# ScalarE's weight casts ahead of its sixteen copies, and GpSimd's value weights ahead of its sums

## The reference

```
h_q = rmsnorm(layernorm(x)) @ w_q.T      h_k = ctx @ w_k.T      h_v = ctx @ w_v.T
score = softmax(mask(h_q h_k^T + position_bias))
x = x + layernorm(x) + (score h_v) @ w_out.T
```

## Time and profile before

| | |
|---|---|
| median of 3 runs | 1126.73 us (1124.93 to 1127.22) |
| profiled execution, its own time | 1123.38 us |
| its span | 1121.6 us, 17499 instructions |
| TensorE busy | 974.0 us, 87% |
| its weight loads | 826.9 us, 74% |
| VectorE busy | 694.0 us, 62% |
| ScalarE busy | 676.8 us, 60% |
| GpSimd busy | 524.9 us, 47% |
| the sixteen copies (L798) | 1024 copies, 303.1 us |
| chain that ended last | TensorE 49%, ScalarE 16%, issue 13%, GpSimd 11%, VectorE 10% |

### The profile page before, as it was taken

One profiled execution on the slowest core, in us unless ns is written; L12 is line 12 of the kernel. 1 busy time (PEld: TensorE's weight loads), 2 busy tenths in 40 slices (PEclk: granted clock), 3 DMA queues, 4 the chain that ended last, 5 costly groups with the idle time before them and its releaser, 6 DMA issues.

```text
span 1121.6 us, 17499 instructions
## 1 busy us (share of the span) xinstructions
PE 974.0 (87%) x5261; PEld 826.9 (74%) x5261; DVE 694.0 (62%) x1225; ACT 676.8 (60%) x2103; POOL 524.9 (47%) x582
## 2 busy tenths in 40 slices
PE   9899999979888888979888888888897987879998
PEld 8778888867767667767777677776786776657886
DVE  5576665556666566747655565647555555748687
ACT  5786856564656474757655565746655465635565
POOL 2443443563537254744446352745446442403367
PEclk9999999999999899989989989989989989989999
DMA  8142267445662546526553546426643553420101
GB/s 309 62 149 100 95 238 253 175 132 188 205 232 73 199 151 224 173 75 229 201 197 116 201 139 221 137 99 218 215 169 131 188 168 120 128 107 1 30 20 57
DMA packets 61292, 171.71 MB, mean 153 GB/s; under 512 B 6055, under 2 KB 8491, under 8 KB 60988
## 3 DMA queue, kind: packets, MB, share of 16 engines
q1 hardware_dynamic: 61244, 171.11, 44.0%
HBM read 159.56 MB, written 11.53 MB: 153 GB/s over the span
## 4 chain that ended last, share of the span: by engine, by line
PE 49%; ACT 16%; issue 13%; POOL 11%; DVE 10%; DMA 0%; DVEq 0%; POOLq 0%; SPq 0%; ACTq 0%
ACT probs_t L798 9%; PE ps_v L363 5%; PE ps_v L365 4%; PE ps_v L364 4%; PE ps_o L363 3%; PE ps_k L363 3%; PE ps_o L364 3%; PE ps_o L365 3%; PE ps_k L364 3%; PE ps_k L365 3%; PE ps_s L2188 3%; PE ps_q L363 3%; ACT scores L787 3%; PE ps_q L364 3%; PE ps_q L365 2%
## 5 line engine op out<-in xcount | busy, mean ns | idle before, releaser
L798 ACT COPY probs_t<-scores 32x128 f32<-32x128 f32 x1024 | 303.1, 296 | 215.4 <-DVE scores L1612 203.6
L787 ACT ACTIVATE scores<-scores,neg_max 128x128 f32<-128x128 f32 x256 | 99.6, 391 | 128.6 <-DVE neg_max L1598 128.0
L1484 DVE TENSOR_TENSOR acc<-ps_o,acc 128x512 f32<-128x512 f32 x128 | 87.7, 685 | 67.1 <-PE ps_o L365 67.1
L1159 POOL TENSOR_TENSOR wq_lo<-raw_q,wq_hi 128x256 fp32r<-128x256 f32 x65 | 53.6, 825 | 144.5 <-ACT wq_hi L620 144.5
L1594 DVE TENSOR_TENSOR scores<-ps_s,shift 128x512 f32<-128x512 f32 x64 | 44.3, 691 | 119.0 <-PE ps_s L2188 115.7
L363 PE MATMUL ps_o<-wo_hi,att_hi 128*128 128x512 f32 x256 | 106.4, 416 | 7.0 <-DVE acc L1484 5.2
L363 PE MATMUL ps_v<-wv_hi,ct_hi 128*128 128x256 f32 x264 | 81.0, 307 | 31.4 <-POOL wv_lo L1205 21.1
L364 PE MATMUL ps_o<-wo_lo,att_hi 128*128 128x512 f32 x256 | 103.6, 405 | 0.0
L365 PE MATMUL ps_o<-wo_hi,att_lo 128*128 128x512 f32 x256 | 102.8, 402 | 0.0
L363 PE MATMUL ps_v<-wv_hi,ring_hi 128*128 128x256 f32 x144 | 48.4, 336 | 51.9 <-POOL wv_lo L1205 42.4
L1472 DVE TENSOR_TENSOR att_lo<-ps_t,att_hi 128x512 fp32r<-128x512 f32 x64 | 44.2, 691 | 76.2 <-ACT att_hi L781 76.2
(11 more groups left out here) (393 smaller groups left out, 2917.6 us busy)
## 6 DMA issues: line engine op xcount, KB each, us to landing
ring_hi<-scratch_x_t SPq DMA_DIRECT2D x39, 512.0 KB, 4.0
ring_lo<-scratch_x_t SPq DMA_DIRECT2D x39, 512.0 KB, 5.0
ring_hi<-scratch_c_t SPq DMA_DIRECT2D x39, 512.0 KB, 5.3
ring_lo<-scratch_c_t SPq DMA_DIRECT2D x39, 512.0 KB, 6.2
raw_o<-in_w_o SPq DMA_DIRECT2D x16, 512.0 KB, 3.3
raw_q<-in_w_q SPq DMA_DIRECT2D x15, 512.0 KB, 3.3
raw_k<-in_w_k SPq DMA_DIRECT2D x15, 512.0 KB, 4.2
xt_hi<-scratch_x_t SPq DMA_DIRECT2D x13, 512.0 KB, 5.5
```

The source lines that it names most:

```text
L787: e = act.activation(probs[n][:, m, :], scores[n][:, m, :], ACT.Exp, bias=neg_max[:, n, m:m + 1], accum_out=row_sum[:, n, m:m + 1])
L798: last = act.copy(block_of(probs_t, j, i), block_of(scores[n], i, j))
L1159: pool.tensor_tensor(w_slot(wq_lo, slot), src, w_slot(wq_hi, slot).bitcast(F32), ALU.subtract).then_inc(wq_lo_s, 1)
L1484: dve.tensor_tensor(acc[:, b, :], ps_o[:], acc[:, b, :], ALU.add).then_inc(o_added, 1)
```

## The change

On ScalarE the sixteen copies of a step of the turns are one call. Ahead of it come now, in the steps that have them: the cast of value weight 3 (in step 0, also ahead of att_hi), of value weight 2 (step 4, ahead of att_hi too), the casts of the sums in steps 0 and 4, `high_second` in steps 1 and 5, and the casts of value weights 4, 1, 6, 7 and 5 in steps 2, 3, 5, 6 and 7.

On GpSimd the subtraction of value weight 3 moves from step 1 to step 0, ahead of `low_first`, and that of weight 4 from step 3 to step 2. Three of the four sums of value weights move from step 5 to step 4, ahead of `rest_o`; the fourth becomes `v_last_sum`, in step 5 behind `low_second`. TensorE, VectorE and SyncE have the same instructions in the same order.

The diff:

```diff
--- before.py
+++ after.py
@@ -846,8 +846,11 @@
                 if c % 4 == 2 and more:
                     k_first(G)
                 exponentials(s, n)
+                if c == 0 and own:
+                    high_v3(i)
                 if c == 4 and coming:
                     v_first(i + 1, 0)
+                    high_v2(i + 1)
                 if c % 4 == 1 and more:
                     q_first(G)
                 attention_high(s - 1)
@@ -858,19 +861,14 @@
                     q_evac(s + 2, 1, 0)
                     k_evac(s + 3, 1, 1)
                 if c == 4 and coming:
-                    high_v2(i + 1)
                     v_first(i + 1, 1)
                 if c % 4 == 0 and more:
                     high_first(G)
+                    high_sums(G)
+                if c % 4 == 1 and more:
+                    high_second(G)
                 if c % 4 == 2 and more:
                     high_third(G)
-                pt_blocks(s, n, (0, 1))
-                if plain:
-                    split_v(PLAIN)
-                if c % 4 == 0 and more:
-                    high_sums(G)
-                if c == 0 and own:
-                    high_v3(i)
                 if c == 2 and own:
                     high_v4(i)
                 if c == 3 and coming:
@@ -881,11 +879,11 @@
                     high_v7(i + 1)
                 if c == 7 and coming:
                     high_v5(i + 1)
-                pt_blocks(s, n, (2, 3))
+                pt_blocks(s, n, (0, 1, 2, 3))
+                if plain:
+                    split_v(PLAIN)
                 if c % 4 == 0:
                     split_o(g)
-                if c % 4 == 1 and more:
-                    high_second(G)
                 if plain:
                     q_evac(s + 3, 1, 1, ps_q2)
 
@@ -1214,6 +1212,8 @@
                 pool.tensor_tensor(v_sum[:], v_odd[1][:], v_even[0][:], ALU.subtract).then_inc(v_sum_s, 1)
                 pool.wait_ge(v_sum_s, 4 * p + 2)
                 pool.tensor_tensor(v_even[1][:], v_even[1][:], v_sum[:], ALU.subtract).then_inc(v_sum_s, 1)
+
+            def v_last_sum(p):
                 pool.tensor_tensor(v_odd[0][:], v_odd[0][:], v_odd[1][:], ALU.add).then_inc(v_sum_s, 1)
 
             def rebuild(w, chunks, cols):
@@ -1272,10 +1272,14 @@
                         pool.wait_ge(wide_t, 8)
                     weight_sums(G, 0, raw_q, wq_in)
                     weight_sums(G, 1, raw_k, wk_in)
+                if c == 0 and own:
+                    low_v(i, 6, 0, v_even[1][:])
                 if c == 4 and coming:
                     low_v(i + 1, 2, 0, v_even[1][:])
                 if c % 4 == 0 and more:
                     low_first(G)
+                if c == 4 and coming:
+                    v_sums(i + 1)
                 if last and c == 4:
                     for m in range(NC):
                         if m == NC - 1:
@@ -1288,21 +1292,20 @@
                     rest_o(g)
                 if first:
                     rest_v(PLAIN)
-                if c == 1 and own:
-                    low_v(i, 6, 0, v_even[1][:])
                 if c == 5 and coming:
-                    v_sums(i + 1)
                     low_v(i + 1, 3, 1, v_sum[:])
                 if c % 4 == 1 and more:
                     low_second(G)
+                if c == 5 and coming:
+                    v_last_sum(i + 1)
                 if c % 4 == 2 and more:
                     low_third(G)
+                if c == 2 and own:
+                    low_v(i, 7, 0, v_odd[1][:])
                 if c == 6 and coming:
                     low_v(i + 1, 4, 0, v_even[0][:])
                 if c % 4 == 3 and more:
                     low_fourth(G)
-                if c == 3 and own:
-                    low_v(i, 7, 0, v_odd[1][:])
                 if c == 3 and coming:
                     low_v(i + 1, 1, 1, v_even[0][:])
                 if c == 7 and coming:
```

## The result

The changed kernel takes 1005.31 us (median of 4 runs, 1004.35 to 1006.55) against 1126.39 of the kernel before (4 runs): a ratio of 0.8927, 95% interval 0.8911 to 0.8942. The forecast was 999 us, so the gain is 121 us in place of 128. Its profiled execution took 1006.55 us with a span of 1004.8 and a mean granted clock of 0.993; the busy times are TensorE 929.7 us (93%), VectorE 702.9, ScalarE 672.0, GpSimd 525.9.

What follows compares the result with a forecast made beforehand. TensorE sets the pace, waiting for wv_lo four times a turn, which also lowers its clock. 21.7 us a turn times 5 is 108.5, plus 13.2 and 6.3 outside: 128.0 off, 999 us; own range 980 to 1020, eight in ten 978 to 1050.

Steps and rivals of the forecast that it cites:

- outside the five turns: Rest of the run beyond the five full turns: 13.2 us from the waits and 6.3 from the clock.
- Steps 1, 3 and 5: TensorE's waits for value weights there, 3.48, 3.99 and 3.41 us a turn, were all to go.
- Step 6: TensorE's wait for the value weight of cast 7: of 4.24 us a turn, 1.46 were to stay.
- The four waits together: TensorE's waits for wv_lo in steps 1, 3, 5 and 6: 15.12 us a turn, less 1.46 that stay.
- The clock: TensorE's granted clock, 0.93 over the five turns, was to recover: 0.07 x 123.9 = 8.7 us a turn.
- Step 0: Cast 3 ahead of att_hi delays VectorE's chain and TensorE's wait for vv: 0.62 us a turn charged, between 0 and 1.3.
- step 4: Cast 2 ahead of att_hi there was to cost nothing, covered by two more products that TensorE has to do.
- the third rival: GpSimd's work contends with VectorE's softmax, 2.64 us a step if in all 56 steps: 1147 us, slower; chance 0.03.
- The first rival: Remaining short TensorE waits of 1.5 and 1.6 us also lower the clock, 2.2 us a spell: 1025 us; chance 0.14.
- The row of 1.93 us: Profile row where TensorE's clock stood at 1.00 after a 1.93 us wait; the prediction's evidence against the first rival.

Runs made afterwards that it cites:

- cast3_behind: Changed kernel with ScalarE's cast of value weight 3 put back behind att_hi in step 0, GpSimd's order kept: 1015.03 us, ratio 0.9006.
- no_collide: Changed kernel with GpSimd made to wait at three places until VectorE is past its own softmax instruction: 987.18 us, ratio 0.8753.
- act_half: ScalarE's half of the change alone, GpSimd's order as in the kernel before: 1074.73 us, ratio 0.9525.
- pool_half: GpSimd's half of the change alone, ScalarE's order as in the kernel before: 1069.84 us, ratio 0.9493.
- weight7_later: Changed kernel with the seventh value weight of step 6 subtracted one GpSimd instruction later, behind the next shift: 1016.07 us, ratio 0.9014.
- no_collide_w7: no_collide plus step 6's seventh value weight cast and subtracted ahead of the third query and key casts and rests: 978.13 us, ratio 0.8666.
- sums_first: no_collide_w7 with VectorE's two value additions of step 0 ahead of its softmax's second part: 974.90 us, ratio 0.8644.

## Why the prediction was right, and what it mis-sized

The mechanism held: TensorE waited for four late value weights a turn, three of these waits went, and the clock rose with them. Against the profiled times, 116.8 us were gained (1123.38 to 1006.55) where 128.0 were summed; outside the five turns it was 116.8 - 5 x 19.33 = 20.2, forecast 19.5. What is short lies in the turns: 19.3 for 21.7.

- Steps 1, 3 and 5: no wait is left for a value weight, as forecast. In step 5 the three sums did fill the time in which GpSimd idled for wo_hi, 2.42 us before and 0.32 now:

```profile
535.27 2.40 POOL L1107 TENSOR_TENSOR wo_lo<-raw_o,wo_hi 128x1024 fp32r<-128x1024 f32 x1 [0.32 <-ACT wo_hi L717]
```

- Step 6: 1.6 us stay, forecast 1.46. The four waits together gave back 15.12 - 1.61 = 13.5 us, forecast 13.66.
- The clock is the largest mis-sized term: 8.7 a turn, measured 7.3. The prediction took 0.07 of the whole turn, 123.9 us. Unrounded, the granted clock before was 0.934, which makes 8.2; and a slow clock stretches only the time in which TensorE works. Added up over the trace, 81.9 us of the five turns were at the 1.2 GHz level, TensorE was busy in 75.3 of them, and half of that is 37.7 us, 7.5 a turn.
- Step 0: charged 0.62, measured 1.32 - 0.98 = 0.34. The reason given was wrong as well: VectorE's chain is not later. Its addition vv, first before and then now:

```profile
523.81 0.68 DVE L1557 TENSOR_TENSOR vv<-ps_v,vv 128x512 f32<-128x512 f32 x1
...
478.95 0.68 DVE L1560 TENSOR_TENSOR vv<-ps_v,vv 128x512 f32<-128x512 f32 x1
```

  That is 11.67 us behind the start of the step (512.14) and 11.40 (467.55). The cast ahead of att_hi does cost 0.5 us there, as cast3_behind shows, but the chain gains as much elsewhere, as the charge's lower bound, zero, had it. It is TensorE that comes sooner: its wait for the copies fell from 0.81 to 0.21 us, and 0.60 less 0.27 is the 0.33 by which the wait for vv grew.
- New waits outside step 0 were not priced. The listed waits other than for value weights were 0.19 + 0.81 + 0.98 + 0.60 + 0.76 + 0.40 = 3.74 us in the turn before from 512.14, and are 5.20 in the turn above: 1.46 more, where only 0.62 were charged. Those of steps 1, 3 and 7 (0.92 + 1.19 + 0.58 = 2.7) are the contention that no_collide removes. The 0.66 of step 4, where the prediction saw a cover, comes with ScalarE's half: such waits for ScalarE's vv make 4.2 us in act_half and 0.8 in pool_half and before. What in that half makes them was not tried.

So 13.5 - 1.46 + 7.3 = 19.3, the turn measured. Contention, the third rival, was a mechanism of this kernel, not of every step: its 1147 us did not come, but it cost 18 us at three places, of the 30.4 that the runs here took off the changed kernel. The reason against it, that the same instructions met before, does not hold for these places. In the kernel before, the instructions of steps 1, 3 and 7 that now take 1.72 to 1.75 us were undisturbed. The change moved the collisions more than it added to them: VectorE's three softmax instructions took 65.1 + 32.5 + 23.9 us for 64 steps before, and 73.7 + 33.1 + 24.9 after.

The first rival, short waits that cool, did not come true in the five turns, where the clock is 1.00, but the reason against it was too weak. The row of 1.93 us was one case: the same wait, before the same instruction, was followed by 0.66 over 5 us in weight7_later, no_collide_w7 and sums_first. In weight7_later:

```profile
194.76:199.76 5.00, 5.00 (x27) 4.91 (x28) 2.09 (x5) 0.53 (x2) 1.42 (x2) 0.66 0.87 332
```

In act_half all six waits of 1.8 us in step 5 were followed by 0.66 and all six of 1.5 in step 6 by 1.00; in the changed kernel itself two waits of 1.8 us outside the five turns were followed by 0.66. That its waits of 1.3 to 1.6 us in the turns kept the clock was in part luck. Traffic rose to 203 GB/s, forecast 209.

## What to carry to other kernels

When instructions move, price what they meet in their new places: look for instructions of the engine next in line that take far longer than their like, and see whether a GpSimd instruction ends where they end. That the same instructions met before is no answer, as they met elsewhere. An added wait on GpSimd can be a gain, if GpSimd has idle time and VectorE's chain has none. Reckon a clock's loss on the part of the slow time in which TensorE is busy, and try two halves of a change apart before calling one of them the cause.

## What the runs showed of the hardware

In the changed kernel's turn VectorE's negation of 128x4 took 1.72 us for 0.17, and its multiply 1.74 and 1.75 for 0.69, ending 0.03 and 0.54 to 0.55 us behind a GpSimd instruction. GpSimd can be the one that is late: its wk_lo at 477.12, with the multiply of step 0 beside it until 477.70, took 1.18 us for 0.72. Keeping GpSimd out at three places took VectorE's three softmax instructions from 131.7 to 99.7 us.

The length of a wait alone does not tell whether the clock falls. All six waits of 2.7 to 2.85 us in step 6 of weight7_later left it at 1.00; of equal waits of 1.78 us in cast3_behind some left it at 1.00 and some were followed by 0.74. In the kernel before, waits of 3.4 to 4.2 us were mostly followed by 0.5 to 0.7, but three of 3.4 us by 5 us at 1.00. What else decides, these runs do not settle.
